# Attention denominators of the first layer: exponentials added over the key tiles on GpSimd, one product with ones per group

## What is computed

```python
def _L0_cond_ref(x, mask, Wq, Wo):
    xt = jnp.transpose(x, (0, 2, 1))
    q = xt @ Wq.T
    qh = q.reshape(B, T, NH, dk).transpose(0, 2, 1, 3)
    scores = scale * jnp.einsum('bhqd,bhkd->bhqk', qh, qh)
    logits = (scores * cmask + (1.0 - cmask) * NEG) * rmask
    attn = jax.nn.softmax(logits, axis=-1)
    ctx = jnp.einsum('bhqk,bhkd->bhqd', attn, qh)
    out = ctx.transpose(0, 2, 1, 3).reshape(B, T, D) @ Wo.T
    return jnp.transpose(out, (0, 2, 1))
```

## Time and profile before

| | us |
|---|---|
| median of 3 runs | 3319.63 (3316.03 to 3322.01) |
| profiled execution, its own time | 3319.23 |
| its span, first to last instruction | 3317.4 |
| first layer, about | 0 to 818 |
| recurrent layer, about | 818 to 2100 |
| second attention, about | 2100 to 3317 |

### The profile page before, as it was taken

The page is one execution under the profiler, slowest core; times in us unless marked ns, Lnnn a source line. Parts: engine busy times, 40 slices in busy tenths (PEclk is TensorE's granted clock), DMA queues, the critical chain, the costliest instruction groups (busy, mean ns, idle before and its releaser), DMA issues. The chain is left out here.

```text
span 3317.4 us, 118574 instructions
## 1 busy us (share of the span) xinstructions
PE 2930.1 (88%) x48920; PEld 1639.8 (49%) x48920; DVE 1953.0 (59%) x4155; ACT 1254.5 (38%) x2019; POOL 644.7 (19%) x717
## 2 busy tenths in 40 slices
PE   6999999996599999999999999389998898888983
PEld 2333333332488888888888888233333232323320
DVE  4555555551776767667676753466666566566650
ACT  1445444443011111111111111136665566656663
POOL 0000000000011212112121211123333343333422
PEclk7999999998799999999999999779999999999996
DMA  1211101111000000000000000144544454554522
GB/s 54 83 47 46 45 26 42 45 36 34 6 0 0 0 0 0 0 0 0 0 0 0 0 0 0 63 123 135 158 141 143 142 155 135 142 151 136 161 58 63
DMA packets 135604, 196.95 MB, mean 59 GB/s; under 512 B 24134, under 2 KB 88870, under 8 KB 129218
## 3 DMA queue, kind: packets, MB, share of 16 engines
q1 hardware_dynamic: 122786, 189.08, 19.4%
q10 hardware_dynamic: 12672, 6.29, 0.6%
HBM read 125.73 MB, written 69.58 MB: 59 GB/s over the span
## 5 line engine op out<-in xcount | busy, mean ns | idle before, releaser
L1289 DVE TENSOR_REDUCE x<-bank 128x1 f32<-128x512 f32 x1024 | 645.0, 684 | 339.4 <-PE bank L1358 338.5
L1213 ACT ACTIVATE x<-exp_ps 128x1024 f32<-128x1024 f32 x512 | 508.6, 1020 | 287.4 <-PE exp_ps L1332 285.2
L807 PE MATMUL exp_ps<-region,gru_hT 128*16 128x128 f32 x16384 | 495.5, 273 | 0.4 <-DVE gru_hT L897 0.4
L1358 PE MATMUL bank<-region 100*128 100x512 bf16 x1024 | 411.1, 404 | 65.3 <-DVE x L1289 40.4
L807 PEld LDWEIGHTS exp_ps<-region,gru_hT 128*16 128x16 f32 x16384 | 431.3, 103 | 19.5 <-DVE gru_hT L897 1.2
L1332 PE MATMUL exp_ps<-region 103*128 103x512 bf16 x1024 | 399.7, 397 | 3.4 <-ACT x L1213 2.3
L869 DVE SCALAR_TENSOR_TENSOR xT<-x,condT,xT (+1 forms) x480 | 358.4, 795 | 0.0
L842 ACT ACTIVATE gru_r<-exp_ps 128x128 f32<-128x128 f32 x256 | 71.2, 278 | 748.6 <-PE exp_ps L807 748.6
L515 DVE TENSOR_REDUCE l_maxes<-exp_ps 128x2 f32<-128x1024 f32 x176 | 215.3, 1225 | 221.3 <-PE exp_ps L576 220.0
L1347 PE MATMUL bank<-x 128*17 128x512 f32 x2048 | 280.2, 620 | 65.1 <-ACT x L1197 64.6
L741 POOL TENSOR_TENSOR xT<-xT,gru_hT 128x64 f32 (+1 forms) x256 | 134.2, 524 | 993.9 <-DVE gru_hT L897 649.2
(11 more groups left out here) (136 smaller groups left out, 3760.9 us busy)
## 6 DMA issues: line engine op xcount, KB each, us to landing
key_query_scratch<-x SPq DMA_DIRECT2D x192, 256.0 KB, 3.4
region<-key_query_scratch SPq DMA_DIRECT2D x64, 768.0 KB
l_rden<-rden_scratch SPq DMA_DIRECT2D x64, 256.0 KB
l_out<-x_scratch SPq DMA_DIRECT2D x64, 192.0 KB
l_xin<-in_x SPq DMA_DIRECT2D x16, 512.0 KB, 4.5
l_rden<-rden_scratch SPq DMA_DIRECT2D x128, 64.0 KB, 2.0
l_xres<-in_x SPq DMA_DIRECT2D x16, 512.0 KB, 3.8
x_scratch<-x SPq DMA_DIRECT2D x16, 512.0 KB, 8.2
```

The source lines that it names most:

```text
L807: last = pe.matmul(out[QW * j:QW * j + rows, cols], hT[:, p, k, 0:rows], wh[:, k, j, gate, :], start=False, stop=True, skip_group_check=True)
L1213: act.activation(probs[:, 2 * (seg % 2) + hp, :, :], exp_ps[slot % 2][:, :, :], ACT.Exp)\
L1289: dve.tensor_reduce(maxes[:, half, qt, head % HH:head % HH + 1], tasks.bank(n)[:, :], AX_X, ALU.max)\
L1358: last = pe.matmul(out, stack[0:KMAX, 1 - par, 1, head, qt * P:qt * P + P], stack[0:KMAX, 1 - par, 0, head, :], start=True, stop=True)
```

## The change

GpSimd adds the exponentials of a group's four tiles of keys, two heads at a time: for kt = 1, 2, 3 and both hp one add of 128x1024 f32, twelve in a step, into psum, a tile of SBUF in a spare part of region. The ones-products are then made once for each group, of the sum, four products in slot 2 (group 1 of the step before) and slot 10 (group 0) instead of four in every odd slot. probs grows from two segments to four, ctx_sb moves into the spare part of region. The exponential now waits for the weighted sums of four segments before (o_done) and for the add that has read its buffer (added); the first add of a group waits for the denominators of the group before (d_done). mta moves from slot 10 to 9, the reciprocal from 5 to 7, the scales from 9 and 12 to 10 and 13, the copies of the denominators (evac_den) from 2 and 10 to 3 and 11.

```diff
@@ -227,15 +227,19 @@
     scale = 1.0 / math.sqrt(D0)
     SLOTS = 16
 
-    AT = {"mtb": 1, "q1": 3, "v1": 5, "mta": 10, "q0": 11, "v0": 13, "out": 15, "reciprocal": 5, "sums": 10}
-    SCALE = (9, 12)
+    AT = {"mtb": 1, "q1": 3, "v1": 5, "mta": 9, "q0": 11, "v0": 13, "out": 15, "reciprocal": 7, "dens": 2}
+    SCALE = (10, 13)
     SEGS = 8
     NPART = 4
     with ExitStack() as ctx:
         sb = lambda name, shape, dt: ctx.enter_context(nc.sbuf_tensor(name, shape, dt))
         sem = lambda name: ctx.enter_context(nc.semaphore("l0_" + name))
 
-        probs = sb("l0_probs", [P, 4, 2, T], F32)
+        probs = sb("l0_probs", [P, 8, 2, T], F32)
+
+        spare = Arena(g.region[:, 4 * TC * TC * GATES * P:])
+        psum = spare.take([P, GH, T], F32)
+        ctx_sb = spare.take([P, 2, CC, T], F32)
         xin = sb("l0_xin", [P, CC, T], F32)
         xres = sb("l0_xres", [P, CC, T], F32)
         mask_bc = sb("l0_mask_bc", [P, T], F32)
@@ -251,7 +255,6 @@
 
         max_rows = sb("l0_max_rows", [P, 2, T], BF16)
         key_rows = sb("l0_key_rows", [P, 2, T], BF16)
-        ctx_sb = sb("l0_ctx", [P, 2, CC, T], F32)
         den_sb = sb("l0_den", [P, T], F32)
         den_c = sb("l0_den_c", [P, H0 * T // P], F32)
         rden_bc = sb("l0_rden", [P, T], F32)
@@ -271,7 +274,7 @@
         ready = {k: sem(k + "_ready") for k in kinds}
         taken = {k: sem(k + "_taken") for k in kinds}
         kq_done = [sem("kq0_done"), sem("kq1_done")]
-        o_done, pv_done = sem("o_done"), sem("pv_done")
+        o_done, d_done, added = sem("o_done"), sem("d_done"), sem("added")
         split_chain, split_done, masks_set = sem("split_chain"), sem("split_done"), [sem("masks_lo_set"), sem("masks_hi_set")]
         o_taken, d_taken = sem("o_taken"), sem("d_taken")
         recip_done, ctx_ready = sem("recip_done"), sem("ctx_ready")
@@ -381,10 +384,28 @@
                                  g.condT[:, :, bass.ds(b, 1)].rearrange("p k (o u) -> p k o u", u=1).broadcast_to([P, TC, GH, 1]))\
                     .then_inc(masks_set[half], 1)
 
+            def add_tile(s, seg, hp):
+
+                grp, kt = seg // 4, seg % 4
+                n = 12 * s + 6 * grp + 2 * (kt - 1) + hp
+                out = psum[:, 2 * hp:2 * hp + 2, :]
+                wait(pool, taken["st"], 16 * s + 2 * seg + hp + 1)
+                if kt == 1:
+
+                    wait(pool, d_done, 2 * s + grp)
+                    pool.tensor_tensor(out, probs[:, hp, :, :], probs[:, 2 + hp, :, :], ALU.add).then_inc(added, 1)
+                else:
+                    wait(pool, added, n - 1)
+                    pool.tensor_tensor(out, out, probs[:, 2 * kt + hp, :, :], ALU.add).then_inc(added, 1)
+
             def step(s, par):
                 if active(s, 1):
                     set_masks(0, "mta", s + 1)
                     set_masks(1, "mtb", s + 1)
+                if active(s, 0):
+                    for seg in (1, 2, 3, 5, 6, 7):
+                        for hp in range(2):
+                            add_tile(s, seg, hp)
 
             pool.wait_ge(spread_set, 1)
             pipeline(pool, step, LAST + 1)
@@ -409,7 +430,7 @@
             def evac_v(idx, kind, b, par):
                 wait(act, ready[kind], b + 1)
 
-                wait(act, pv_done, SEGS * (b - 2) + 4 * (idx + 1))
+                wait(act, o_done, SEGS * (b - 2) + 4 * (idx + 1))
                 act.activation(v_sb[:, par, :, idx * P:idx * P + P],
                                tasks.bank_of(kind)[:, 0, :].rearrange("p (k o) -> p k o", k=TC), ACT.Copy)\
                    .then_inc(taken[kind], 1)
@@ -432,7 +453,7 @@
 
             def evac_den(s, grp):
 
-                wait(act, pv_done, SEGS * s + 4 * (grp + 1))
+                wait(act, d_done, 2 * s + grp + 1)
                 wait(act, den_stored, 16 * (2 * s + grp))
                 act.activation(den_sb[:, :], d_ps[:, :], ACT.Copy).then_inc(d_taken, 1)
 
@@ -441,15 +462,16 @@
                     seg, hp = slot // 2, slot % 2
                     if active(s, 0):
 
-                        wait(act, pv_done, SEGS * s + seg - 1)
+                        wait(act, o_done, SEGS * s + seg - 3)
+                        wait(act, added, 12 * s + 6 * (seg // 4 - 1) + 2 * max(seg % 4 - 1, 0) + hp + 1)
                         wait(act, ready["st"], 16 * s + slot + 1)
-                        act.activation(probs[:, 2 * (seg % 2) + hp, :, :], tasks.bank_of("st", slot)[:, :, :], ACT.Exp, scale=scale)\
+                        act.activation(probs[:, 2 * (seg % 4) + hp, :, :], tasks.bank_of("st", slot)[:, :, :], ACT.Exp, scale=scale)\
                            .then_inc(taken["st"], 1)
                     if isinstance(s, int) and s in (0, 1):
                         load_gru_weights(SLOTS * s + slot)
                     if slot == 1 and active(s, -1):
                         evac_sums(s - 1, 1 - par, 1)
-                    if slot == 2 and active(s, -1):
+                    if slot == AT["dens"] + 1 and active(s, -1):
                         evac_den(s - 1, 1)
                     if slot == AT["mtb"] and active(s, 0):
                         evac_max(1, "mtb", s)
@@ -459,9 +481,9 @@
                         evac_v(1, "v1", s + 1, 1 - par)
                     if slot == AT["mta"] and active(s, 1):
                         evac_max(0, "mta", s + 1)
-                    if slot == AT["sums"] - 1 and active(s, 0):
+                    if slot == 9 and active(s, 0):
                         evac_sums(s, par, 0)
-                    if slot == AT["sums"] and active(s, 0):
+                    if slot == AT["dens"] + 9 and active(s, 0):
                         evac_den(s, 0)
                     if slot == AT["q0"] and active(s, 2):
                         evac_q(0, "q0", s + 2)
@@ -593,18 +615,16 @@
                 for j in range(GH):
                     h = GH * grp + j
                     last = pe.matmul(o_ps[QW * j:QW * j + QW, :], v_sb[:, par, kt, h * D0:h * D0 + D0],
-                                     probs[:, 2 * (seg % 2) + j // 2, j % 2, :], start=(kt == 0), stop=(kt == TC - 1))
+                                     probs[:, 2 * (seg % 4) + j // 2, j % 2, :], start=(kt == 0), stop=(kt == TC - 1))
                 last.then_inc(o_done, 1)
 
-            def denominators(s, par, seg):
-
-                grp, kt = seg // 4, seg % 4
-                if kt == 0:
-                    wait(pe, d_taken, 2 * s + grp)
+            def denominators(s, grp):
+
+                wait(pe, added, 12 * s + 6 * (grp + 1))
+                wait(pe, d_taken, 2 * s + grp)
                 for j in range(GH):
-                    last = pe.matmul(d_ps[QW * j:QW * j + QW, :], ones[:, :], probs[:, 2 * (seg % 2) + j // 2, j % 2, :],
-                                     start=(kt == 0), stop=(kt == TC - 1))
-                last.then_inc(pv_done, 1)
+                    last = pe.matmul(d_ps[QW * j:QW * j + QW, :], ones[:, :], psum[:, j, :], start=True, stop=True)
+                last.then_inc(d_done, 1)
 
             def task(s, par, n, kind):
                 out = tasks.bank(n)
@@ -651,11 +671,14 @@
                             tasks.free(pe, s, n)
                             task(s, par, n, kind)
                     seg = slot // 2 - 1
-                    part = denominators if slot % 2 else weighted_sums
-                    if seg >= 0 and active(s, 0):
-                        part(s, par, seg)
-                    if seg < 0 and active(s, -1):
-                        part(s - 1, 1 - par, SEGS - 1)
+                    if slot % 2 == 0 and seg >= 0 and active(s, 0):
+                        weighted_sums(s, par, seg)
+                    if slot % 2 == 0 and seg < 0 and active(s, -1):
+                        weighted_sums(s - 1, 1 - par, SEGS - 1)
+                    if slot == AT["dens"] and active(s, -1):
+                        denominators(s - 1, 1)
+                    if slot == AT["dens"] + 8 and active(s, 0):
+                        denominators(s, 0)
 
             pipeline(pe, step, LAST + 1)
 
```

## The result

The changed kernel takes **3358.23 us** (median of 4 runs, 3357.48 to 3362.41), the kernel before 3318.99 beside it; ratio 1.0121, 95% interval 1.0103 to 1.0138. I had forecast 3303.5, range 3284 to 3326. The profiled execution took 3362.41 (span 3360.6), 43 more than before's. The recurrent layer starts at about 859 instead of 818, so the layers behind it lost little (under 3 us of the 43).

A forecast was written before the change was run, and what follows sets the result against it. Bound: TensorE's own work, competing with its wait for ScalarE's exponential. Full step -2.12 + 1.04 = -1.08, 13 steps -14.0; with steps 0 (-1.8), 14 (+0.2) and 15 (-0.1) -15.8 from 3319.23: 3303.5, range 3284 to 3326.

The forecast's parts named there:

- DMA chain: DMAs behind the moved reciprocal and scales: den_c has 7 us of slack, the first scale 2; no cost in the sum.
- (c): Rival, slots 3 and 11: lagging adds hold kq beyond about 0.7, at full size 2.0, 3344; chance 0.15 in part or whole.
- a granted clock under 1.00 between 100 and 700 us: Sign of being wrong in another way, in steady attention's stretch of the trace; given no chance.
- Step 15: The last step, without max products: -0.1 us as an estimate.
- TensorE and ScalarE: Full step's schedule: denominators out of odd slots -3.59, mta +0.17, groups in slots 2 and 10 +0.77 and +0.53: -2.12.
- The hold in slot 7: GpSimd's add holds the split's first subtract 1.66 us on VectorE, delaying slot 10: +1.04 a step, bounds 0 and 1.3.
- The full step without the late x: Full step: -2.12 + 1.04 = -1.08 against 46.04; 44.96 forecast.
- The coin of slot 13: Scale of slot 13 and an add ready almost together; taken as won, if lost the output task waits 0.52.
- An add of 2.13: GpSimd's 128x1024 f32 add takes 2.13; twelve are 25.6 of a step of 44, so the sum is not late.
- The step before the last: Step 14, no q0 and v0, exponential bounds both kernels: -2.12 + 1.28 + 1.04 = +0.2.
- (a): Rival: nothing on VectorE is held, the port is only shared; -31.4, 3288; chance 0.27.
- (b): Rival: the scale in slot 13 is held by the add, 14 x 0.52 = 7 back, 3310.5; chance 0.22.

The follow-up runs named there:

- before_late_x: The kernel before with only the reciprocal in slot 7 and the scales in slots 10 and 13: 3349.7 us, ratio 1.0089.
- x_early: The changed kernel with SyncE's loads of x, mask and keys issued ahead of the wait for the reciprocal: 3336.3 us, ratio 1.0049 to the kernel before.
- direct_tail: x_early_split_first with the last two steps' denominators made as in the kernel before, a group in each odd slot, no GpSimd adds there: 3321.6 us.
- direct_tail2: direct_tail with ScalarE's copy of the denominators' bank back in slots 2 and 10 for the last two steps: 3295.7 us, ratio 0.9922 to the kernel before.
- after_fill_last: The changed kernel with five groups of ones-products that nobody reads in the last step's slots 5, 7, 9, 13 and 15: 3373.1 us.
- x_early_no_adds: x_early with each add cut to 2x8 columns and the denominators' product made from the last key tile alone: 3312.0 us, ratio 0.9971 to the kernel before.
- x_early_split_first: x_early with GpSimd's second add of each group's last key tile waiting until VectorE's split is done: 3312.4 us, ratio 0.9977 to the kernel before.
- x_early_mta10: x_early with mta back in slot 10, where the kernel before has it: 3332.2 us.
- all_three: x_early_split_first with ones-products that nobody reads added in the last two steps: 3303.3 us, ratio 0.9960 to the kernel before.

## Why the prediction was wrong

**The step that failed first** is one sentence: "DMA chain: the reciprocal moves two slots later, the scales one each; den_c has 7 us of slack, the first scale 2". I asked who needs the reciprocal, and not what else stands behind it in SyncE's queue. x for the next projection does, with a margin that the move used up. The held split of slot 7, ahead of the reciprocal, delays it further; what part of the wait is its share no run separates, and before_late_x waits 2.36 to 2.95 without it. Alone in the kernel before the late x costs 1.79 a step and 29 us in all; taken out of the changed kernel it gives 22. None of my rivals had it, and the one that came out near the measured time, (c) with 3344, had another mechanism: kq took 1.48, held by 0.79 and not by 2.0, and cost nothing.

**The second** is the clock: "a granted clock under 1.00 between 100 and 700 us, which I give nothing", and "Step 15 has no max products, -0.1 as an estimate". The sum takes work away from TensorE in a layer in which TensorE showed 100 us busy of 100 at a clock of 1.00; it had no term for what the clock would do then. The last step cost +16.9 and not -0.1, each of the falls in the steady steps of x_early 1.65. What the clock costs in a last step is shown by direct_tail and direct_tail2: the same instructions, one copy moved, 0.50 against 1.00, 64.85 against 40.98. For the changed kernel's own last step it is read from its slots (2.46 at the upper level, 3.53 to 4.11 at the lower); no run has that step, without its odd groups, at 1.00 throughout. (A filling that starts after the fall, in after_fill_last, does not undo it.)

**The rest of the sum held.** TensorE and ScalarE: -2.12 forecast, -2.12 measured (x_early_no_adds, x_early_split_first). That it agrees to the last digit is luck: in x_early_split_first the slots that I had at 2.48 take 2.42 (v) and 2.45 (1 and 9), and the plain slots 4, 12 and 14 2.30 or 2.31 instead of 2.27, errors that mostly cancel. The hold in slot 7: +1.04 forecast, +1.11 measured; it caught the cast where I had it on the subtract, 2.40 instead of 0.20, which stood in my upper bound ("1.3 if the cast before it is held as well"), and mta started about 1.5 late, not 1.16. The full step without the late x and at the upper level: 44.96 forecast, 44.99 measured. The coin of slot 13 fell as taken (four scales of 0.69 on average between 300 and 400). The coin's price, where it was lost (x_early_mta10), was 0.56 for 0.52. An add of 2.13 was 2.40; the sum was not late for its product, as I said.

**The step before the last**, +0.2 forecast with the hold in it: 44.82 in x_early, +0.15, where the clock stays at 1.00 in this step; but 47.84 in the changed kernel, where the clock falls in it (752 to 759).

One line on the chances does not add up: the forecast, (a) and "a good half of (b)" are 0.31 + 0.27 + 0.11 or more, at least 0.69, and not 0.65.

The Trainium skill (SBUF — State Buffer, section Who interferes with whom) says that casts may enter a mode that takes the shared port as well, and that who issues first keeps it. The trace agrees: the cast of 128x16 f32 to bf16 that began just behind an add took 2.40, and 0.20 in x_early_split_first, where no add lay over it.

**What stays open**: why a wait of some 2.5 us brings the clock down in one place and not in another. before_late_x has one of 2.36 to 2.95 in each of twelve steps at 1.00, and fell behind one of 4.36; x_early has one of 2.25 to 2.36 in each of twelve and fell in five; all_three has three of 2.52 in its last two steps and in its profile kept 1.00 until 770; direct_tail fell behind its second. In the changed kernel's last step it fell at 779 without a wait over 1.05 among TensorE's loads since 766. So no single length of a wait tells it, and the runs don't show what does.

## What to carry to other kernels

Before moving a wait on a queue that issues DMAs, list what is issued behind it, not only who uses its result: x, which came late here, does not depend on what was moved. When work is taken from the engine that sets the time, look for the places where it was what kept that engine busy, first at the ends of a pipeline, where other work has run out, and leave it there. And where a long GpSimd instruction with slack holds a small VectorE instruction on the critical path, as here, let the small one go first: one wait gave 24 us.

## What the runs showed of the hardware

- A GpSimd add of 128x1024 f32 takes 2.40 us in place and 2.35 with two other inputs, both from SBUF, where the second attention's took 2.13. Why, no run here tells.
- A VectorE cast of 128x16 is held like an instruction with two inputs: 2.40 instead of 0.20, until the add's end. A reduce out of PSUM is not: the 120 that begin under an add in the changed kernel take 1.22 to 1.23, as in the steady steps before.
- After the fall, the granted clock came back within some 3.4 us in a steady step (369.0 to 372.4 in x_early), but not for 47 us in the last step of direct_tail, though TensorE shows 45.32 us busy in these 47 and gets the same work as in direct_tail2. A slot takes 4.11 there (750.34 to 754.45, from one small load L600 to the next), 2.17 to 2.51 in direct_tail2's last step behind the output task.
